# Delta-rule phase: a projection moved between two small products, unread products inside the joins and in the end rounds, and no clearing at the seam behind it

## The reference

```
x = x + delta_rule_attention(attention_with_bias(x, mask))
x = x + mixture2(mixture1(x, cond))
```

```
q, k, v = short_conv(h @ Wq), short_conv(h @ Wk), short_conv(h @ Wv)      # 4 taps, then SiLU
q, k = mix * rotary(q) + (1 - mix) * q, the same for k;  q, k = l2norm(q), l2norm(k)
beta, gamma = sigmoid(h @ Wb), sigmoid(h @ Wgamma)
v, kb = v * beta, k * beta
A = -(kb @ k.T) * strict_lower            # 32 x 32 in each chunk
T = inverse of (I - A);   u = T @ v;   w = T @ kb
for each chunk:                            # in order, S is 64 x 64 for each head
    u_t = u - w @ S
    o   = q @ S + (q @ k.T * lower) @ u_t
    S   = mean(gamma) * S + k.T @ u_t
core = rmsnorm(o) @ Wo
out  = core + sigmoid(h @ Wg + b) * rmsnorm(fractal_mixer(h))
```

## Time and profile before

| | us |
|---|---|
| median of 3 runs (lowest to highest) | 2613.3 (2605.02 to 2617.29) |
| the profiled execution, its own time | 2598.78 |
| its span in the trace | 2596.9 |
| delta phase in that span: first issue to last work | 1099.07 to 1742.14 |
| mean granted clock of PE over the span | 0.962 |

### The profile page before, as it was taken

How to read it: one execution, slowest core, us unless ns; L and a number is a source line. 1 busy time by engine, 2 the same in 40 slices (tenths; PEclk the granted TensorE clock), 3 DMA queues, 4 the chain that set the end, 5 groups by cost and what they waited for, 6 DMA issues and landing times. The chain is left out here.

```text
span 2596.9 us, 55676 instructions
## 1 busy us (share of the span) xinstructions
PE 2384.3 (92%) x20326; PEld 1958.1 (75%) x20326; DVE 1739.9 (67%) x4114; ACT 1223.7 (47%) x3111; POOL 1337.3 (51%) x1465
## 2 busy tenths in 40 slices
PE   4999999999999999857999999978899999999998
PEld 3788888888888888735777777756677878778786
DVE  4576776767677777577788878326755846747664
ACT  2666665666666666455455555114333333332332
POOL 3676776767676767346556656214422322322322
PEclk8999999999999999978899999889999999999999
DMA  4000100000000000001121121216112112212211
GB/s 141 7 10 9 45 18 10 9 10 10 10 10 9 9 5 5 15 15 38 39 55 43 44 54 46 51 57 178 33 54 70 58 44 72 66 42 62 65 39 58
DMA packets 156686, 105.00 MB, mean 40 GB/s; under 512 B 85168, under 2 KB 134832, under 8 KB 156416
## 3 DMA queue, kind: packets, MB, share of 16 engines
q1 hardware_dynamic: 131072, 62.83, 9.0%
q10 hardware_dynamic: 25344, 38.60, 4.9%
HBM read 80.51 MB, written 20.88 MB: 39 GB/s over the span
## 5 line engine op out<-in xcount | busy, mean ns | idle before, releaser
L920 POOL TENSOR_TENSOR a_bm<-a_bias,a_mask_add 128x512 f32<-128x512 f32 (+3 forms) x512 | 438.3, 872 | 190.1 <-DVE a_nm L674 184.9
L1529 POOL TENSOR_TENSOR m_hid_part<-m_hid,m_hid_part 128x512 fp32r<-128x512 f32 x176 | 240.2, 1365 | 564.0 <-ACT m_hid_part L1438 560.9
L830 ACT ACTIVATE a_S<-a_S,a_nm 128x512 f32<-128x512 f32 (+3 forms) x512 | 289.2, 565 | 346.3 <-DVE a_nm L674 343.6
L674 DVE CUSTOM_DVE_ANT_0 a_S<-a_S,a_bm,a_nsn 128x512 f32<-128x512 f32 (+3 forms) x512 | 275.5, 545 | 140.3 <-PE a_S L438 136.0
L461 PE MATMUL a_O<-a_v,a_PT 128*128 128x64 f32 x2560 | 342.4, 265 | 0.0
L461 PEld LDWEIGHTS a_O<-a_v,a_PT 128*128 128x128 f32 x2560 | 328.4, 193 | 0.1
L1450 ACT ACTIVATE m_hid<-m_G 128x512 f32<-128x512 f32 x176 | 105.4, 599 | 408.7 <-PE m_G L1384 370.9
L438 PE MATMUL a_S<-a_kT,a_qT 128*128 128x384 f32 (+3 forms) x1024 | 283.9, 358 | 3.5 <-DVE a_nm L674 3.0
L1611 DVE TENSOR_TENSOR m_hid<-m_hid,m_U 128x512 f32<-128x512 f32 x176 | 121.0, 688 | 223.3 <-PE m_U L1384 189.6
L1401 PE MATMUL m_Y<-m_hid_part,m_down_high 128*128 128x512 f32 x704 | 257.4, 407 | 12.4 <-POOL m_hid_part L1529 11.1
L1384 PE MATMUL m_G<-m_in,m_gate_high 128*128 128x512 f32 x704 | 251.9, 398 | 2.6 <-POOL m_up_low L1523 1.6
(11 more groups left out here) (314 smaller groups left out, 5264.2 us busy)
## 6 DMA issues: line engine op xcount, KB each, us to landing
m_spread<-s_w ACTq DMA_DIRECT2D x64, 256.0 KB, 3.3
m_spread<-s_w ACTq DMA_DIRECT2D x128, 128.0 KB, 2.9
a_x<-in_x SPq DMA_DIRECT2D x32, 128.0 KB, 2.1
s_hT<-a_hT SPq DMA_DIRECT2D x32, 128.0 KB, 2.1
d_x<-in_x SPq DMA_DIRECT2D x8, 512.0 KB, 5.4
d_h<-s_hT SPq DMA_DIRECT2D x8, 512.0 KB, 5.7
s_xg<-d_xg SPq DMA_DIRECT2D x8, 512.0 KB, 3.1
d_x<-s_xg SPq DMA_DIRECT2D x8, 512.0 KB, 4.7
```

The costliest lines, as they stand in the source:

```text
L674: dve.tensor_tensor_reduce(S[:, n % S_SLOTS, 0:w], SB[n % 2][:, 0:w], bm[:, n % BM_SLOTS, 0:w], -1.0, nsn[:, tile % 2, h:h + 1], ALU.add, ...
L830: act.activation(S[:, n % S_SLOTS, 0:w], S[:, n % S_SLOTS, 0:w], ACT.Exp, scale=-1.0, bias=nm[:, tile % 2, h:h + 1], accum_out=den[:, tile ...
L920: pool.tensor_tensor(bm[:, n % BM_SLOTS, 0:w], bias[:, h, L - w:L], mask_add[b % 2][:, 0:w], ALU.add).then_inc(s["bm_ready"], 1)
L1529: pool.tensor_tensor(hid_part[1][:, q % H_SLOTS], hid[:, q % G_SLOTS], hid_part[0][:, q % H_SLOTS].bitcast(F32), ALU.subtract).then_inc(hi ...
```

## The change

It has five parts.

1. In `PE_ROUND` proj(5) and M(0) change places: proj(5) now stands behind step 2, M(0) behind step 3. `ACT_ROUND` follows: M(0)'s copy stands behind z(0)'s.
2. Unread products: M(3) issues none any more. Z and TZ issue two ahead of their work where they issued one, and two more at j = 5 (on the 352 columns of the bank that aren't written yet) and two at j = 10 (192 columns). The four pieces qkT of batch 2 issue two each.
3. `fast` also stands behind steps 12 to 15 of batch 5's recurrence (round 7), with three products each.
4. Each of the four `hold` pieces issues four instead of two.
5. The delta phase's semaphores are made in `bass_adaln`, so `clear` behind that phase goes, and they are cleared by the last `clear` of the kernel. SP no longer waits for the last x1 stores at the end of the delta phase, but in the mixture phase behind the weight loads, and no longer for hT's stores at the end of the attention phase, but ahead of the first load of h in the delta phase.

The diff, cut to its core:

```diff
-                for i in range(TT):
-                    sp.wait_ge(hT_out[i], 16 * B)
...
                 for m, part, s, _, src, dst in units:
                     sp.dma_start(dst, src).then_inc(w_in[m][part][s], 16)
+                sp.wait_ge(x1_out, 16 * B)
...
-            if 0 <= r - lag < B and not (name == "fast" and r - lag < B - 2) and not (name == "hold" and r - lag < B - 1):
+            if 0 <= r - lag < B and not (name == "fast" and r - lag < (B - 3 if i >= NCH - 4 else B - 2)) and not (name == "hold" and r - lag < B - 1):
...
-        DENSER = {("M", 3), ("M", 0), ("Z", 0), ("TZ", 0)}
+        DENSER = {("M", 0): 1, ("Z", 0): 2, ("TZ", 0): 2}
+        N_FAST = {**{(B - 1, i): 1 for i in range(NCH)}, **{(B - 2, i): 3 for i in range(NCH)},
+                  **{(B - 3, i): 3 for i in range(NCH - 4, NCH)}}
...
-            ("step", 2, R), ("fast", 2, R), ("M", 0, R), ("au", 1, R), ("z", 0, IN),
-            ("step", 3, R), ("fast", 3, R), ("proj", 5, IN), ("z", 1, IN), ("au", 2, R), ("mixer", 1, F),
+            ("step", 2, R), ("fast", 2, R), ("proj", 5, IN), ("au", 1, R), ("z", 0, IN),
+            ("step", 3, R), ("fast", 3, R), ("M", 0, R), ("z", 1, IN), ("au", 2, R), ("mixer", 1, F),
...
-            ("M", 0, R), ("silu", 3, IN), ("z", 0, IN),
-            ("proj", 5, IN), ("z", 1, IN), ("frac", 1, F),
+            ("silu", 3, IN), ("proj", 5, IN), ("z", 0, IN),
+            ("M", 0, R), ("z", 1, IN), ("frac", 1, F),
...
+                        if bi == 0:
+                            for i in range(TT):
+                                sp.wait_ge(hT_out[i], 16 * B)
...
-                sp.wait_ge(x1_out, 16 * B)
...
-                    if (name, i) in DENSER:
-                        unread(o, 1)
+                    unread(o, 2 if (name, b) == ("qkT", 2) else DENSER.get((name, i), 0))
                     return o
 
-                def unread(o, n):
+                def unread(o, n, at=0):
 
                     rows = causal[:].bitcast(mybir.dt.bfloat16)
                     for _ in range(n):
-                        pe.matmul(o[:, :].rearrange("p (a n) -> p a n", a=2), rows[:, 0:P],
-                                  rows.unsqueeze(1).broadcast_to([P, 2, 2 * P]), start=True, stop=True)
+                        pe.matmul(o[:, at:].rearrange("p (a n) -> p a n", a=2), rows[:, 0:P],
+                                  rows[:, 0:(L - at) // 2].unsqueeze(1).broadcast_to([P, 2, (L - at) // 2]), start=True, stop=True)
...
                     elif name == "fast":
-                        unread(fill(name, i, b), 1 if b == B - 1 else 3)
+                        unread(fill(name, i, b), N_FAST[b, i])
...
-                        unread(fill(name, i, b), 2)
+                        unread(fill(name, i, b), 4)
...
                         for j in range(TT * H2):
+                            if j in (5, 10):
+                                unread(o, 2, j * CH)
...
-        clear(nc, sems)
```

More of the change, by code:

```diff
@@ L135, in mixture_inputs, with attention_phase @@
     return t
-def attention_phase(nc, a, ident, delta, mixture, bias_rows, hT_dram, inv_dram):
+def attention_phase(nc, a, ident, delta, mixture, hT_out, bias_rows, hT_dram, inv_dram):
     QK_LAG, PV_LAG, S_SLOTS, PT_SLOTS = 2, 4, 5, 3
@@ L262, in attention_phase @@
         mask_loaded = [sem(f"mask_loaded{i}") for i in range(2)]
-        hT_out = [sem(f"hT_out{i}") for i in range(TT)]
         FRONT = {"stat": -5, "xn": -3, "xT": -2, "q0": 0, "q1": 1, "kv": 2, "ss": 3, "qn": 4, "kT": 7,
@@ L1002, in rank_below, with mixtures_phase @@
     link(dve.tensor_scalar(out, out, float(k), None, ALU.is_lt))
-def mixtures_phase(nc, a, ident, mixture, shared_sems, x1_dram, w_dram, out):
+def mixtures_phase(nc, a, ident, mixture, kept_sems, x1_out, x1_dram, w_dram, out):
     F32R = mybir.dt.float32r
@@ L1660, in _ @@
                         route(*part)
-        clear(nc, sems + shared_sems)
+        clear(nc, sems + kept_sems)
 def pieces(table):
@@ L1667, in pieces, with delta_phase @@
         for name, i, lag in table:
-            if 0 <= r - lag < B and not (name == "fast" and r - lag < B - 2) and not (name == "hold" and r - lag < B - 1):
+            if 0 <= r - lag < B and not (name == "fast" and r - lag < (B - 3 if i >= NCH - 4 else B - 2)) and not (name == "hold" and r - lag < B - 1):
                 yield name, i, r - lag
-def delta_phase(nc, a, ident, delta, mixture, hT_dram, xg_dram, low_dram, inv_dram, x1_dram):
+def delta_phase(nc, a, ident, delta, mixture, hT_out, sem, x1_out, hT_dram, xg_dram, low_dram, inv_dram, x1_dram):
     PAD = DELTA_PAD
@@ L1678, in delta_phase @@
     with ExitStack() as ctx:
-        sb, bank, sem, sems = space(nc, ctx, "d")
+        sb, bank, _, _ = space(nc, ctx, "d")
         wqkv, wsm, smb, conv, frac, cos, sin, rot, mixw, strict, causal, chunk_of, side, eye16, corner, wo, onw, x = (
@@ L1823, in delta_phase @@
         x1_ready = sem("x1_ready")
-        x1_out = sem("x1_out")
         NS = NCH - 1
-        DENSER = {("M", 3), ("M", 0), ("Z", 0), ("TZ", 0)}
+        DENSER = {("M", 0): 1, ("Z", 0): 2, ("TZ", 0): 2}
+        N_FAST = {**{(B - 1, i): 1 for i in range(NCH)}, **{(B - 2, i): 3 for i in range(NCH)},
+                  **{(B - 3, i): 3 for i in range(NCH - 4, NCH)}}
         PE_ROUND = [
@@ L2543, in bass_adaln @@
         mixture = mixture_inputs(nc, ctx, a, sem)
+        hT_out = [sem(f"hT_out{i}") for i in range(TT)]
+        x1_out = sem("x1_out")
         with ExitStack() as until_delta:
             delta = delta_inputs(nc, until_delta, a, sem)
[L2546 to L2549, removed]
+            attention_phase(nc, a, ident, delta, mixture, hT_out, scratch["bias_rows"], scratch["hT"], scratch["inv"])
+            delta_phase(nc, a, ident, delta, mixture, hT_out, sem, x1_out, scratch["hT"], scratch["xg"], scratch["low"],
+                        scratch["inv"], scratch["x1"])
+        mixtures_phase(nc, a, ident, mixture, sems, x1_out, scratch["x1"], scratch["w"], out)
 def kernel(**inputs):
```

## The result

| | before | after |
|---|---|---|
| median of 7 runs (lowest to highest), us | 2603.8 (2594.1 to 2617.3) | 2580.3 (2580.1 to 2590.4) |
| the profiled execution, its own time (span), us | 2598.78 (2596.9) | 2580.29 (2578.5) |
| mean granted clock of PE in it | 0.962 | 0.972 |

The ratio is 0.9917, 95% interval 0.9892 to 0.9942: 21.6 us faster, give or take 6.5. Of the 20.7 us between 2601 and 2580.3, 9.5 are the level it was set on (three runs of before had a median of 2613.3, the seven of this comparison 2603.8). The other 11.2 are the size of the change: 12.3 on that level, 23.5 between the two medians.

The account below looks back on a forecast made before the run. PE was taken to bound the delta phase's steady rounds. Costs of 12.3 us against gains of 24.4 (clock, tail, seams) net -12.1: 2586.7 on the profiled execution, 2601 on the median, range 2584 to 2618.

Parts of the forecast that it names:

- round 2's 6 us: Delta phase, round 2: the 24 us low-clock stretch from 1245 us goes, gaining 6 us.
- the cost sum of 12.3 us: Added PE work in the delta phase: joins 9.8, qkT of batch 2 2.0, round 7's steps 12 to 15 0.5.
- Two joins are 1.76 to 2.16 us a round: Z and TZ, rounds 2 to 8: added products' price per round, before M(3)'s 0.32 back; 9.8 us taken, bounds 6 to 13.
- Round 8 and the tail: Low-clock stretch from 1620.5 us goes, gaining 7.5 us; last batch's norm and core matmuls gain 2.4 (bounds -0.7 and +2.7).
- Round 7 ... 0.5 net: Products behind steps 12 to 15: 3.0 us of work, mostly in PE's waits; 0.5 net cost, bounds 0 and 3.0.
- The rival in which one long stretch stays: Products go in but one or both 24 us low-clock stretches stay: -4.6 us without the 7.5, +1.4 without both; chance 0.33.
- Short stretches: Delta phase: four low-clock windows of 3.5 to about 7 us, about 1 us each in their rounds, gaining 4 us.
- the pair of the earlier trace: Stretch from the product ahead of M(0) to transposes z(1): 6.19 us at full clock, 8.91 where it fell; about 6 expected.
- Pure cost: Joins' products only add work, idle gaps lower the clock and products around gaps don't close them: +8 to +12.5 us; chance 0.10.
- The seams: Both ends of the delta phase: landing waits 2.6 and 1.5 us go, clearing gives 0.4; gain 4.5 us.
- The rival that explained the 14.5 us between profile and median by more stretches: Timed runs hold further low-clock stretches that the change also removes: -26 us, 2587; chance 0.12.
- the likeliest case: All or nearly all low-clock stretches gone: 2601 us, own range 2592 to 2608; chance 0.45.

Follow-up runs that it names:

- seam_alone: Kernel before with only part 5 (delta-phase semaphores cleared at the kernel's end, two landing waits moved): 2592.9 us, ratio 0.9967.
- no_join_products: Changed kernel with Z and TZ back to one leading unread product each and none inside: 2576.0 us, ratio 0.9890.
- seam_swap_ends: Kernel before with parts 1, 3, 4 and 5; no new products in joins or qkT, M(3) keeping its own: 2575.4 us, ratio 0.9895.
- join_narrow: Kernel before with parts 1, 3, 4, 5 and M(3)'s product, plus two 32-column products at j = 5 and j = 10 of both joins: 2578.7 us, ratio 0.9900.
- no_end_products: Changed kernel without products behind steps 12 to 15 of batch 5 and with two per hold piece: 2597.7 us, ratio 0.9974.

## Why the prediction was wrong in size and right in kind

The split puts the forecast's terms beside what was measured (us; minus is faster):

| term | forecast | measured |
|---|---|---|
| clock, all parts | -19.9 | -16.8 |
| work: seams | -4.5 | -4.5 |
| work: products in the joins, M(3)'s left aside | +12.0 | +7.2 and +6.6 |
| work: qkT of batch 2 | +2.0 | -0.9 and -0.7 |
| work: exchange | 0 | -2.4 and -2.5 |
| work: ends | +0.5 | +0.7 and -1.1 |
| work in all, M(3)'s product (forecast -2.2) in it | +7.8 | -1.3 |
| sum | -12.1 | -18.1 (means: -17.9; ratio: -21.6) |

- **Bound and mechanism: right.** The gain is the clock's: 0.9610 to 0.9709, at 0.33 us for each low-clock microsecond, the third that the earlier trace rows had given. That the sum of the clock terms is right within 3.1 us is in part luck: round 2's 6 us didn't come, and the end products' clock is worth 13 (taken out) to 14 us (put in) where 9.9 had been expected.
- **The failed step is the cost sum of 12.3 us,** "Two joins are 1.76 to 2.16 us a round", over rounds 2 to 8. The single join was priced too low (1.20 against at most 1.08), but the sum too high. The forecast let PE's waits take up 10% or so of it; they took up half, 8.9 of 16.8 us, 5.4 of it in gaps inside the joins. The trace had shown the larger share: the earlier trace rows were read as a sign of how the clock falls, and not as 5.6 us that inner products might fill. The round of 69.95 us, too, from which the worth of short stretches was read, holds the longest of these gaps, 1.94 us. The rival's sentence that such products "don't close them" is wrong for inner ones, and half right for those ahead: they leave 2.2 us of gaps.
- **The small costs** went the same way: qkT's 2.0 aren't seen, and the exchange, priced at nothing, saves 2.4 us of work in both directions of the test. M(3)'s product was priced right as far as can be told (2.3 for 2.2). Together with the joins they make up the 9 us by which the work was off. Why the exchange saves work beyond the clock is open.
- **Round 8 and the tail: right in the profile.** Round 8 is 6.0 us shorter and the tail 2.0. Over many executions the end steps' products give -7.0 alone (7.5 forecast, less 0.5 of cost); the held ones' -1.6 (2.4) can't be told from nothing, and both together give 14.8, more than the forecast's sum of 9.4. "Round 7 ... 0.5 net" held: round 7 became no longer.
- **Round 2: wrong.** The 6 us there didn't come. The stretch stands earlier, at the turn from round 1, and neither the joins' products nor qkT's raise the mean clock in the whole change. The rival in which one long stretch stays described this, with its sum for the other stretch: 4.6 us gained in all, or 6.1 by the forecast's 6 for round 2. Neither fits, since the work term was better than forecast.
- **Short stretches: about half.** They are 13 us in rounds 3 to 6, 21 before. The forecast said that the pair of the earlier trace rows should read about 6 us in every round with proj between; in the new order proj isn't between them, so the row couldn't answer.
- **Pure cost** describes the joins' products and nothing else: in the whole change they are 7.2 us without a gain of clock. Alone they raise it by 0.0033, worth 5.6 us, and nearly earn back what they cost (6.6).
- **The seams** were sized right in sum, by luck, since two errors cancel: more went at the seam (4.8 and 1.6) and 2.2 came back at the end, where 0.4 net had been allowed. The other half of what seam_alone gains is clock (0.0027), within its noise.
- **The level.** The rival that explained the 14.5 us between profile and median by more stretches took the scatter of three runs for a property: with seven runs that distance is 5.0, with the 88 others 3.0. The ends of the likeliest case's own range don't follow from its terms either: costs of 15 give 2604 and not 2608, and the doubled gains 2595 and not 2592.

Of the versions run, no_join_products and seam_swap_ends have the lowest ratios, 0.9890 and 0.9895, with 0.9917 for the changed kernel. The intervals overlap; that the joins' products should go rests on the work term, which shows it from both sides, and on the means (8.3 us less without them).

## What to carry to other kernels

An edit that is meant for the clock is judged by the mean granted clock of many executions and by the time at equal clock, since the stretches in one profile move with every shift, and in the combination in which it is to stay: here the parts' clock gains alone were 0.0163 in sum and 0.0099 together. Put unread work where the matrix engine waits anyway (here behind the last steps of round 7, with no cost to be seen and for 7 us), not into a piece that bounds the round. And before work is added to a run of tiny instructions, look for gaps in it with no releaser: they are time that the addition may fill.

## What the runs showed of the hardware

- Runs of 128 matmuls on 32 x 32 tiles, 10 ns each, hold gaps of 0.4 to 1.9 us in which nothing is issued, in the kernels without inner products mostly in the same joins and there with the same number of matmuls left. Inner products of 352 and 192 columns close them.
- Full-array products between 32 x 32 ones lengthen the join by 0.25 to 0.30 us for each interruption, beside their columns (2.72 against 2.21 us, 2.13 against 1.52). In the time of join_narrow this doesn't show.
- PE busy without a gap is no protection: 44.5 of 44.5 us busy at 1.2 GHz in no_end_products, and in the 20 us ahead of that stretch, at 2.4 GHz, PE was idle for 0.23 us. The Trainium skill (TensorE: Matmul & The Clock Gate, HAM oscillation) names idle gaps between groups as what throttles the engine; this stretch has none in it, and the fall does not agree with that rule. What in the mix of instructions ahead of a stretch brings the clock down wasn't isolated.
